# A DLRM tower on one core: the gram products of a tile in four parts instead of eight, three units turned early instead of four

## What is computed

```python
    e = jnp.stack([tbl_0[ids[:, 0]], ..., tbl_31[ids[:, 31]]], axis=1)   # 2048 x 32 x 256
    dots = jnp.einsum('bnd,bmd->bnm', e, e)
    z = dots[:, iu, ju]                                    # 496 pairs i < j
    h = jnp.concatenate([z, dense_ctx], axis=1)            # 512
    h = jnp.maximum(h @ W_top1 + b_top1, 0.0)              # 512
    h = jnp.maximum(h @ W_top2 + b_top2, 0.0)              # 256
    return h @ W_top3                                      # 1
```

## Time and profile before

| what | value |
|---|---|
| median of 3 runs | 562.49 us (560.96 to 564.6) |
| the profiled execution | 561.54 us |
| its span (first to last instruction) | 559.8 us |
| TensorE matmul busy, weight loads busy | 503.2 us (90%), 463.9 us (83%) |
| GpSimd busy | 398.3 us (71%) |
| VectorE, ScalarE busy | 229.4 us (41%), 203.5 us (36%) |
| GpSimd's 419 gathers, from first to last start | 2.79 to 530.04 us |

### The profile page before, as it was taken

How to read it: one execution, slowest core, us unless ns; L and a number is a source line. 1 busy time by engine, 2 the same in 40 slices (tenths; PEclk the granted TensorE clock), 3 DMA queues, 4 the chain that set the end, 5 groups by cost and what they waited for, 6 DMA issues and landing times.

```text
span 559.8 us, 24184 instructions
## 1 busy us (share of the span) xinstructions
PE 503.2 (90%) x11019; PEld 463.9 (83%) x11019; DVE 229.4 (41%) x578; ACT 203.5 (36%) x369; POOL 398.3 (71%) x426
## 2 busy tenths in 40 slices
PE   0765999999998999989998998999899998989986
PEld 0755889898997989889897987999798998989984
DVE  3574552533335353433535243353623434341222
ACT  1785160523406051330706133070613416061342
POOL 6777577777777777777777777777777777777700
PEclk9997999999999999999999999999999999999999
DMA  8999444344444344443444444443444443333300
GB/s 193 262 256 308 130 118 123 114 118 119 130 118 123 117 117 120 120 125 116 125 115 118 116 122 125 117 127 118 119 118 114 125 122 118 112 107 106 108 10 2
DMA packets 37460, 70.97 MB, mean 127 GB/s; under 512 B 10383, under 2 KB 23439, under 8 KB 37359
## 3 DMA queue, kind: packets, MB, share of 16 engines
q0 software_dynamic: 20112, 54.95, 34.4%
q1 hardware_dynamic: 17246, 14.48, 10.3%
HBM read 69.39 MB, written 0.01 MB: 124 GB/s over the span
## 4 chain that ended last, share of the span: by engine, by line
PE 70%; POOL 10%; DMA 9%; issue 6%; ACT 4%; DVE 1%; ACTq 0%; DVEq 0%
PE look_ps L340 28%; PE quad_ps L360 15%; POOL rows L297 10%; DMA rows<-in_tbl,row_ids 8%; PE top_ps L409 8%; PE turn_ps L324 6%; PE quad_ps L324 6%; PE top_ps L422 4%; PE quad_ps L379 1%; ACT turned L490 1%; PE top_ps L399 1%; ACT ahead L497 1%; ACT area L519 1%; ACT turned L508 0%; DVE one_hot L684 0%
## 5 line engine op out<-in xcount | busy, mean ns | idle before, releaser
L297 POOL DMA_INDIRECT rows<-in_tbl,row_ids x419 | 397.5, 949 | 131.9 <-issue 119.1
L340 PE MATMUL look_ps<-one_hot,small 125*128 125x256 f32 (+1 forms) x1536 | 221.9, 294 | 6.6 <-DVE small L674 6.1
L340 PEld LDWEIGHTS look_ps<-one_hot,small 125*128 125x128 f32 x1536 | 196.1, 194 | 10.2 <-issue 7.6
L684 DVE TENSOR_SCALAR one_hot<-ids_across,sub_row 125x256 fp32r<-125x256 int32 (+1 forms) x384 | 116.1, 373 | 118.1 <-PE look_ps L340 112.0
L360 PE MATMUL quad_ps<-turned 128*32 128x31 f32 x7680 | 101.9, 199 | 0.4
L360 PEld LDWEIGHTS quad_ps<-turned 128*32 128x32 f32 x7680 | 84.7, 111 | 20.1 <-issue 0.9
L497 ACT ACTIVATE ahead<-look_ps 128x512 f32<-128x512 f32 (+1 forms) x48 | 28.3, 589 | 195.2 <-PE look_ps L340 195.2
L324 PE MATMUL turn_ps<-ident,rows 128*128 128x128 f32 x424 | 62.7, 281 | 22.2 <-DMA rows<-in_tbl,row_ids 22.2
L324 PE MATMUL quad_ps<-ident,rows 128*128 128x128 f32 x414 | 61.2, 279 | 12.8 <-DMA rows<-in_tbl,row_ids 11.7
L324 PEld LDWEIGHTS turn_ps<-ident,rows 128*128 128x128 f32 x424 | 47.4, 142 | 25.5 <-issue 12.4
L324 PEld LDWEIGHTS quad_ps<-ident,rows 128*128 128x128 f32 x414 | 46.2, 142 | 16.1 <-DMA rows<-in_tbl,row_ids 13.4
(11 more groups left out here) (50 smaller groups left out, 157.7 us busy)
## 6 DMA issues: line engine op xcount, KB each, us to landing
rows<-in_tbl,row_ids POOLq DMA_INDIRECT x419
ids_across<-in_small_ids SPq DMA_DIRECT2D x45, 128.0 KB
landed<-in_tbl SPq DMA_DIRECT2D x6, 896.0 KB
w_sb<-in_W_top SPq DMA_DIRECT2D x4, 256.0 KB, 9.7
landed<-in_tbl SPq DMA_DIRECT2D x6, 104.0 KB
w_sb<-in_W_top SPq DMA_DIRECT2D x1, 512.0 KB, 13.1
area<-in_dense_ctx SPq DMA_DIRECT2D x16, 8.0 KB
row_ids<-in_ids SPq DMA_DIRECT2D x1, 240.0 KB, 13.5
```

Of the source, the lines that this page charges most:

```text
L297: pool.indirect_dma_start(out=rows[:, n % PLACES, j, :], out_offset=None, in_=tables[f], in_offset=bass.IndirectOffsetOnAxis(ap=row_ids[:, ...
L340: last = pe.matmul(look_ps[:, c * width:(c + 1) * width], small[:, f, r, part, c * P:(c + 1) * P], one_hot[n % 2][:, r, 0:width], start=(r ...
L684: last = dve.tensor_scalar(one_hot[n % 2][:, r, 0:width], ids_across[0:SP, n % IDS_RING, 0:width], sub_row[:, r:r + 1], None, ALU.is_equal)
```

## The change

Two numbers of the interleaving change.

```diff
-    EARLY_AFTER = [3, 4, 5, 6]
+    EARLY_AFTER = [1, 2, 3]
...
-    PARTS = 8
+    PARTS = 4
     GPP = GROUPS // PARTS
```

## The result

The changed kernel took 579.38 us (median of four runs, 577.26 to 581.42), and the kernel before, run beside it, 561.73 us (560.95 to 564.6). The ratio is 1.0302 with a 95% interval of 1.0261 to 1.0342: slower by 3%. The forecast was 563.1 us and the range ended at 569. The profiled execution shown here took 578.52 us.

What follows compares the result with a forecast made beforehand. GpSimd's stream of gathers was taken as the bound. Steady tiles 0, start +1.2 and last stage -0.6 gave +0.6 us: 562.1 against the profiled execution, 563.1 us against the median; range 559 to 569.

Steps and rivals of the forecast that it cites:

- What bounds the kernel: From some 75 us on, GpSimd's stream of gathers sets the pace at 1.253 us each; TensorE has a little slack.
- The rule that the busiest engine is the bound: Rival: TensorE, 90% busy, is the limit, so each of 14 tiles gains 1.4 us; 543 us, chance 0.03.
- Fewer joints: On TensorE, four borders between gram parts and lookup pieces go, saving 0.6 to 1.6 us per tile, taken as 0.9.
- The slack of unit 3's turn: In steady tiles unit 12's gather is freed 1.8 us before GpSimd reaches it, 0.9 without savings; so no hold-up.
- Both signs of being wrong: In steady tiles, GpSimd gaps ended by a turn, or a granted clock under 1, would show a slow rival right.
- The clock's fall: Longer TensorE waits at tile ends could halve its clock, costing 0 to 1 us per tile; given chance 0.05.
- The rival of the late turn: Unit 3's turn, moved behind the last lookup, holds up unit 12's gather in every tile; +7 us, 570, chance 0.08.
- the rival of the clock: TensorE's granted clock falls in the longer waits at tile ends; up to +14, priced at +7 us, 570, chance 0.05.
- The start: TensorE is late in tile 0, so tile 1's gather of unit 12 goes at 73.96, making the stream 1.2 us later.
- The hole of the earlier trace: A 1.07 us stop in unit 0's turn at 64.42, with no releaser shown, that might also go away.
- The last stage: After the last gather, L399 of tile 15 follows unit 4's turn sooner, so the end gains 0.6 us (0 to 1.3).
- The last lookup's move: The third lookup becomes one piece of 32 behind the last gram part; later copy and picks mostly covered, costed at nothing.

## Why the prediction was wrong

**What bounds the kernel: right.** The end moved with GpSimd's last gather (16.0 of the 16.9 us), and TensorE's waits for rows grew, as was said. The rule that the busiest engine is the bound would again have misled: TensorE's share fell while the kernel became slower.

**Fewer joints, -0.9 us per tile: the sign was wrong.** The joints do go, at 0.16 us each. But a gram portion of 64 products takes 1.77 us (median in after; 1.48 to 2.01 where no stop of over 0.6 us lies in it), and two of 32 take 2 x 0.73 us (median in before). So a tile's grams are 4 x 0.31 = 1.2 us longer, against 4 x 0.16 = 0.6 us saved: +0.6 us per tile. The prediction bounded a joint's cost from below by nothing and never asked whether a long run of these short products goes at the rate of a short one. It should have widened the term to a loss, since no row of before showed more than 32 of them in a row.

**The slack of unit 3's turn, 0.9 to 1.8 us: mis-sized, and so the steady tiles were not free.** The working itself was sound: put +0.6 where it had -0.9, and the 1.8 us become 0.3. After shows it. In tile 6, TensorE lost 4.48 - 3.72 = 0.8 us (unit 12's rows landed 4.48 us after the gather at 207.41, and 3.72 us in the earlier trace rows), 0.4 in unit 12's turn (0.91 us instead of 0.49), 1.1 in layer 1, 2.0 in the hole and 1.5 in the lookup behind it: 5.8 us, and the stream lost 5.7. In tile 8 the same sum is 1.2 + 0.2 + 1.5 + 2.4 + 1.6 = 6.9 us, and the stream lost 6.5. What is not passed on is 0.1 to 0.4 us. Undisturbed tiles indeed cost nothing or up to 0.5 us. Both signs of being wrong that the prediction gave for its slow rivals showed: gaps ended by a turn in steady tiles, and a granted clock under 1 there. The fault was to price the move by one tile without a delay: the 4 us of room that the prediction itself saw being spent are what covers the bad tiles, 0.8 of 3.1 us passed on with early turns and nearly all with the late one.

**The clock's fall: the mechanism was named, and dismissed by a step that failed.** That "a wait for unit 12 alone can hardly be longer than the 2.5 us between two units' rows" took the landing time for constant. The waits were 2.68 and 3.79 us, because rows landed 4.5 and 4.9 us after their gather. The trace of before could have shown it: in tile 9 unit 12's last gather started at 334.86 and its turn, after a wait, at 339.16, which is 4.30 us, where the prediction's one tile had 3.72. The rival of the late turn and the rival of the clock were priced as two cases of 570 us with 0.13 together, each against the other's absence; they act together. A fall of the clock alone cost nothing (one fall with early turns, 0.9997), the late turn of unit 3 at full clock 0.6%, about half of it at the start, and after had both and the holes. The added matmul gave some 11 of the 17.7 us back, and turning all four units early gave back all that can be measured.

**The start, +1.2 us: mis-sized.** It was +3.5 us. Unit 12 of tile 1 was gathered at 76.02 us, where 73.96 was worked out and 72.52 was before. Unit 4's turn began near 75.4 us instead of 73.5, after holes of 1.39 and 1.64 us in tile 0:

```profile
64.29 1.21 PE L340 MATMUL look_ps<-one_hot,small 125*128 125x256 f32 x8 [1.39 <-issue]
...
68.29 0.27 PE L360 MATMUL quad_ps<-turned 128*32 128x31 f32 x8 [1.64 <-issue]
...
72.59 0.66 PE L324 MATMUL turn_ps<-ident,rows 128*128 128x128 f32 x4
...
75.01 1.04 PE L324 MATMUL quad_ps<-ident,rows 128*128 128x128 f32 x8
```

The row at 72.59 is unit 2's turn, and the last row holds the turns of units 3 and 4 together. The hole of the earlier trace rows was counted as something that could go away; it came back twice. The place of the waiting was nearly right: the gathers waited one after the other for units 0, 1 and 2, not for 1, 2 and 3. Unit 2's turn let a gather go at 73.52, and the next unit's followed two steps later, at 76.02; unit 3's turn would have let it go at 75.01 + 0.88 = 75.9.

**The last stage, -0.6 us: wrong by 1.5.** L399's wait went, as worked out: it stands 1.35 us behind unit 4's turn, where it was 1.76. But the stretch behind the last gather is 30.7 us instead of 29.8. From unit 12's turn to the end it is the same (22.2 us, and 22.3 before); TensorE came to unit 4's turn only 2.7 us ahead of the last gather, where it was 4.1. The longer portions and a hole of 1.03 us in tile 14's grams stand ahead of that turn; how much each has was not separated.

**The last lookup's move: right.** The feature transposes no longer wait for `pick`.

**Still open.** Why the rows of unit 12 land later in some tiles. In the bad tiles SyncE's loads of ids and dense numbers stand just ahead of those gathers, instead of behind; this is a correlation and was not tried, and in tile 9 they stand there too, while its rows took 3.76 us and only 0.5 us was held up behind them. And why the same stretch ahead of layer 1 loses the clock in one tile and keeps it in the next. The granted clock also differs between executions of one kernel, and the time with it: of after with early turns in tile 0, the execution with a mean clock of 0.985 took 573.39 us and the one with 0.965 took 581.23.

## What to carry to other kernels

An engine that runs back to back through a ring of buffers is held up by the moment when a place is given back, so a step that gives one back should stand early even when the mean tile has slack behind it; the slack is the cover for the bad tiles, and a change that spends it is priced by the longest delay that a tile can have. When two rivals are each dismissed because the other's condition is missing, they are to be priced together as well. A change that lengthens a run of identical short instructions is to be bounded from the side of loss too, when the trace has no run of that length.

## What the runs showed of the hardware

**TensorE's clock in a stretch of transposes and waits.** Between a tile's last lookup and layer 1 TensorE has only the turns of units 3 or 4 to 12, the features' transposes and waits for rows. The granted clock fell from 1.00 to 0.50 behind such stretches of 8.20 and 9.06 us in after, and stayed at 1.00 behind the ones of 5.0 to 7.5 us in the kernel before. Their length alone does not decide it: the clock fell at one of 7.07 us (eight parts, three late turns) and stayed behind one of 7.76 us (eight parts, four earlier turns). With one 512-column fp32 matmul (a row of 1.02 us) in the stretch, layer 1 ran at 1.00 in every tile of the five kernels that had one. That matmul also shortens the wait behind it (1.45 us at 211.32, where after had 2.68), and no run separates the two. The Trainium skill (TensorE: Matmul & The Clock Gate, Part 4: PE-mode transpose) says of a transpose that it doesn't count as busy in the same way as other work; the falls agree with it as far as they stand behind transposes and waits, but no run has the waits without the transposes, so it is not shown here. The clock also fell at some of the longest holes (0.50 at or behind those of 2.04, 2.25 and 2.40 us), where a hole costs its own length and 0.8 to 1.6 us behind it; at ones of 2.07 us (tile 0 of the kernel with unit 3 alone late) and 2.31 us (after with the matmul) it did not.

**Long runs of short products.** A portion of 64 gram products is 128 matmul and 128 weight load instructions. The kernels with four parts show 15.7 to 19.7 us of stops of the weight loads in 63 to 71 places, the kernels with eight parts 0.7 to 5.5 us in 3 to 8. Holes of 0.7 us and more stand in tile 0 of nearly all the kernels; behind it they occur only in kernels with portions of 64, also where two lookup products break them.

The page's queue of instructions (q8) moves 1.43 MB in 87 transfers. The traces have the time of each, and set beside the holes they show more than the views above: all 46 holes of 0.7 us or more that the 14 traces have from tile 0's grams on end 1.2 to 1.5 us after the end of such a transfer, and a transfer comes only every 6 to 7 us on average. In after, one ran from 235.41 to 236.44 and TensorE went on at 237.83; another ran from 302.53 to 303.53 and TensorE went on at 304.75. So in a hole TensorE stands until its next instructions are there, as far as times can show it; no run changed the supply, and for the many small stops it is not shown. The Trainium skill (Runtime: NRT & Kernel Launch, Instruction fetch mechanics) says that instructions come in blocks of 256, fetched ahead, and that crossing a block is mostly hidden. By that figure 87 blocks are some 22300 instructions (an estimate), close to TensorE's 2 x 11019; the holes are places where the crossing is not hidden.
